# Queries from split operands in a 16-head attention, their weight parts made one layer earlier, and fewer buffers

## The chip, the core and the metric

One core of a Trainium2 chip runs the whole program once. The metric is the device time of one execution in microseconds. PE is the matrix engine, PEld its weight load, DVE, ACT and POOL the vector, scalar and GpSimd engines, SP the engine that issues the DMAs of this kernel.

## What is computed

A residual stream of 4 sequences x 512 tokens x 512 features goes through four pairs of cross-attention and feed-forward; each adds tanh(gate) times its output to the stream. The change touches the third attention and the feed-forward ahead of it. (Beside the third attention the kernel also computes a selective-state recurrence that belongs to the fourth one and doesn't depend on the stream.)

```python
def _L1_ffn_ref(x, w_gate, w_up, w_down):        # ternary weights, 8-bit rows
    gate, up = bitlinear(x, w_gate), bitlinear(x, w_up)
    return h_bitlinear(silu(gate) * up, w_down)  # Hadamard transform of 2048 ahead of it

def _L2_xattn_ref(hidden_states, encoder_hidden_states, Wq, Wk, Wv, Wo, gq, gk):
    q = (hidden_states @ Wq).reshape(B, Sq, H, D)            # H = 16 heads of D = 128
    k = (encoder_hidden_states @ Wk).reshape(B, Skv, H, D)
    v = (encoder_hidden_states @ Wv).reshape(B, Skv, H, D)
    q, k = rmsnorm(q, gq), rmsnorm(k, gk)
    attn = softmax(einsum('bqhd,bkhd->bhqk', q, k) / sqrt(D))
    return einsum('bhqk,bkhd->bqhd', attn, v).reshape(B, Sq, H * D) @ Wo

def step(state, inp):                            # the recurrence, 16 states a channel
    d, b, c, u = inp
    state = state * exp(d[..., None] * A) + (d * u)[..., None] * b[:, None, :]
    return state, einsum('bdn,bn->bd', state, c)
```

## The kernel before

The program is a row of phases (`layer_0`, `l1_xattn`, `l1_ffn`, `l2_xattn`, `moe_and_last`), each with its own buffers, semaphores and one hand-written instruction order per engine; a barrier stands between phases. Every engine runs its list strictly in order, so a wait holds all that follows on that engine. PSUM banks are handed out by `Ring`: jobs take banks in a fixed order, PE fills them, and the job says whether ACT or DVE drains it; a bank is refilled when the job that had it before is drained. Since drains are counted, a wait for one drained job also waits for the jobs of that engine ahead of it in the list.

**The ternary feed-forward, `l1_ffn`.** 16 tiles of 128 tokens go through a pipeline of 19 iterations t (L1591 and the same loop on the other engines). On ACT an iteration does, in this order: copy the turned middle of tile t-1, four SiLUs of tile t (`gate`, L1639), the turned rows of tile t-3 (`y_turned`, L1645), two half copies of tile t-1 (`halves`, L212) and the rounding of tile t-2 (`y_round`). DVE does the Hadamard sums of tile t-2 (`widest`, `rest`, L1734 to L1748), then `middle(t)` and `down(t-3)`, and in every fourth iteration (t = 1, 5, 9, 13) the layer norm for the next sequence, whose power is POOL's only work. SP loads the Hadamard matrix and three weight matrices at the start, waits for two POOL fills, issues one DMA that clears `xs_dram` (L1530; 5888 rows of 513 floats, used two layers later) and waits for it at the end.

**The 16-head attention, `l2_xattn`.** 16 units: 4 sequences x 4 groups of 4 heads (`NU`, `G2`). One iteration u on PE does scores, transposes, values and the output of unit u, and in between the queries, values and keys of units u+1 and u+2 (the order is in the loop that ends the PE block). Keys and values are `split_product`s (L130): both operands are held as a rounded part and a rest in the F32R type, and three products (high x high, high x low, low x high) give one chunk. A query of one head is `product` over 4 chunks in F32: `wq` (1 MB a unit) times `xt`, the transposed normed stream, which `x_turned` copies from PSUM, two chunks by ACT and two by DVE, once for a sequence. ACT squares each query into `q_sq`, copies it to `qt`; the norms follow from a product with ones.

Beside it runs the recurrence, 16 steps (states) a unit: ACT makes `decay`, POOL `inflow` (L2393) and the sum over states (`add_state`, L2405 and L2409), DVE the scan (L2279) and the product with C (`gather`, L2288), and at the end of a unit `skip_term` (L2294), which runs in the next unit behind gather 1. States lie in a circle of `KEPT` = 8 buffers, sums in 2. SP issues two broadcast rows a step, and between them the loads of weights, all on one queue; `inverse` holds two buffers of softmax reciprocals.

Of the kernel before, what the change touches and what calls it, by code (L numbers as in the profile page):

```python
# [5 lines left out]
F32 = mybir.dt.float32  # L6
# [7 lines left out]
P = 128  # L14
# [1457 lines left out]
def l1_ffn(nc, g, a):  # L1472

    with Phase(nc, "l1f") as ph:
# [14 lines left out]
        top = sb("top", [P, 1])  # L1489

# [22 lines left out]
        empty_made, emptied, top_made = sem("empty_made"), sem("emptied"), sem("top_made")  # L1513
        ln = LayerNorm(g, sem)
# [95 lines left out]
        def _(act):  # L1610
# [226 lines left out]
def l2_xattn(nc, g, a):  # L1837

    with Phase(nc, "l2x") as ph:
        sem, sb = ph.sem, ph.sb  # L1840
        wq, wo = [sb(n, [P, DC, D]) for n in ("wq", "wo")]
        wkv = sb("wkv", [P, 2, CC, D], F32R)
        gains = sb("gains", [P, 3])
        ctx_t, xt = sb("ctx_t", [P, 2, CC, S], F32R), sb("xt", [P, DC, S])
        k_tok, v_tok = sb("k_tok", [P, ST, D]), sb("v_tok", [P, ST, D])
        k_sq, q_sq = sb("k_sq", [P, S]), sb("q_sq", [P, 4, S])
# [4 lines left out]
        ot, inv_b = sb("ot", [P, 4, S]), sb("inv_b", [P, 2, S])  # L1851
# [5 lines left out]
        y_sum = sb("y_sum", [P, 2, S])  # L1857
# [12 lines left out]
        b_in, c_in = [[sem(f"{n}_in{k}") for k in range(3)] for n in "bc"]  # L1870
        ln = LayerNorm(g, sem)
# [11 lines left out]
        def _(sp):  # L1883
            def weight(w, name, u, arrived, rows=False):
                cols = slice((u % G2) * D, (u % G2 + 1) * D)
                src = a[name][cols, :] if rows else a[name][:, cols]
                sp.dma_start(w[:], src.rearrange("(c p) n -> p c n", p=P)).then_inc(arrived, 16)
# [41 lines left out]
            weight(wq, "l2_wq", 0, wq_in)  # L1929
# [8 lines left out]
            weight(wo, "l2_wo", 0, wo_in, rows=True)  # L1938
            ring.wait_filled(sp, 0, "q0_3")
            weight(wq, "l2_wq", 1, wq_in)  # L1940
            ring.wait_filled(sp, 0, f"v0_{ST - 1}")
            key_weight(1)
            for u in range(NU):
                for n in range(NS):
                    if n == 3 and u >= 1:
                        ring.wait_filled(sp, 0, f"out{u - 1}_{ST - 1}")
                        weight(wo, "l2_wo", u, wo_in, rows=True)
                    if n == 5 and u >= 1:
                        store_y(u - 1)
                    if n == 8 and u + 1 < NU:  # L1950
                        load_dt(u + 1)
                        load_u(u + 1)
                    if n == 6 and u + 1 < NU:
                        ring.wait_filled(sp, 0, f"k{u + 1}_{ST - 1}")
                        value_weight(u + 1)
                    if n == 10 and u + 2 < NU:
                        ring.wait_filled(sp, 0, f"q{u + 1}_3")
                        weight(wq, "l2_wq", u + 2, wq_in)
# [12 lines left out]
        def _(pe):  # L1971
# [50 lines left out]
            def query(u, h):  # L2022
                if u < NU:
                    pe.wait_ge(wq_in, (u + 1) * 16)
                    ring.wait_for(pe, 0, free=f"q{u}_{h}", drained=[f"xt{u // G2}_{c}" for c in (2, 3)])
                    ring.fill(product(pe, bank(f"q{u}_{h}"), [(wq[:, c, h * P:(h + 1) * P], xt[:, c, :])
                                                              for c in range(DC)]))
# [51 lines left out]
        def _(act):  # L2079
# [25 lines left out]
            def context(u, n, out):  # L2105
                if u < NU:
                    for t in range(ST):
                        ring.wait_filled(act, 0, f"{n}{u}_{t}")
                        if n == "k":
                            for h in range(4):  # L2110
                                cols = slice(h * P, (h + 1) * P)
                                act.activation(k_sq[:, cols], bank(f"k{u}_{t}")[:, cols], ACT.Square,
# [22 lines left out]
            def inverse(u, h):  # L2135
                if u >= 0:
                    ring.wait_filled(act, 0, f"iv{u}_{h}")
                    if u or h >= 2:
                        before = f"pv{u}_{h - 2}" if h >= 2 else f"pv{u - 1}_{h + 2}"
                        ring.wait_for(act, 0, drained=[before])  # L2140
                    copy(act, "act", ring, f"iv{u}_{h}", inv_b[:, h % 2, :], bank(f"iv{u}_{h}"))
# [57 lines left out]
        def _(dve):  # L2199
# [26 lines left out]
            def value(u, h):  # L2226
                if u >= 0:
                    ring.wait_filled(dve, 0, f"pv{u}_{h}")
                    ring.wait_for(dve, 0, drained=[f"iv{u}_{h}"])
                    ring.drain(dve.tensor_tensor(ot[:, h, :], bank(f"pv{u}_{h}"), inv_b[:, h % 2, :], ALU.mult),  # L2230
# [59 lines left out]
            def skip_term(u):  # L2290
                if u >= 0:
                    dve.wait_ge(added, (u + 1) * NS)
                    tile = u_in[:, u % 2, :]
                    dve.scalar_tensor_tensor(tile, tile, g["skip"][:, u % G2:u % G2 + 1], y_sum[:, u % 2, :], ALU.mult,  # L2294
# [65 lines left out]
        def _(pool):  # L2360
# [34 lines left out]
            def add_state(u, n):  # L2395
# [5 lines left out]
                total = y_sum[:, u % 2, :]  # L2401
# [1328 lines left out]
def program(nc, a):  # L3730
    with ExitStack() as stack:
        def sb(name, shape, dt=F32):
# [14 lines left out]
            "kv_dram": nc.dram_tensor("l2x_kv_dram", [3, 4, P, 2 * CC * S], F32).ap(),  # L3747
            "tern_dram": nc.dram_tensor("l1f_tern_dram", [3, P, 4 * I1], BF16).ap(),
# [74 lines left out]
```

## Time and profile before

| | us |
|---|---|
| median of 3 runs | 3502.61 (3500.46 to 3504.72) |
| the profiled execution | 3490.28 |
| its span, first to last instruction | 3488.6 |
| PE busy in the span | 3122.0 |
| DVE busy | 2621.1 |
| ACT busy | 1844.0 |
| POOL busy | 1443.2 |

The ternary feed-forward takes the stretch from about 1077 to 1448 us, the attention that from about 1449 to 2780 us. A timeline row has the start, the duration, the engine, the line, the operation, what it writes and reads, and the count of merged instructions; in brackets stands how long the engine was idle before it, and what ended that.

### The profile page before, as it was taken

What the parts mean: (1) busy time and instruction counts of PE and PEld (TensorE: products, weight loads), DVE (VectorE), ACT (ScalarE), POOL (GpSimd) and SP (SyncE); (2) the same over time, 40 slices, a digit from 0 to 9 for tenths busy, and PEclk for the clock granted to TensorE, in tenths of its full rate; (3) what the DMA queues carried; (4) which work ended last, traced back from release to release, by engine and by line L of the source; (5) the groups of instructions that cost most, each with busy time, mean ns of one, the idle gap of its engine ahead of it and who ended that gap; (6) DMA issues with size and microseconds to landing.
All of it is one profiled execution on the core that took longest, in us unless ns stands there. A gap on an engine that the chain in (4) does not pass through costs nothing. (4 is left out here: it accounts for less than half of the span.)

```text
span 3488.6 us, 42689 instructions
## 1 busy us (share of the span) xinstructions
PE 3122.0 (89%) x14213; PEld 1833.0 (53%) x14244; DVE 2621.1 (75%) x3478; ACT 1844.0 (53%) x3430; POOL 1443.2 (41%) x957
## 2 busy tenths in 40 slices
PE   7869797999997888799999999999999787998985
PEld 3437554333334555455555555555555366786663
DVE  7855689877774888468888888887788864765886
ACT  5644343666663655565666666666656432664220
POOL 1122279000000000067777777777778654223430
PEclk9879899999998999899999999999999898999998
DMA  4137735222216400245555555455454346675421
GB/s 133 40 118 277 277 103 151 58 58 58 64 32 150 63 1 1 85 153 155 182 170 167 162 189 168 154 169 180 159 171 144 127 182 211 249 254 192 145 73 60
DMA packets 229749, 478.66 MB, mean 137 GB/s; under 512 B 36239, under 2 KB 69647, under 8 KB 213664
## 3 DMA queue, kind: packets, MB, share of 16 engines
q1 hardware_dynamic: 223296, 459.19, 41.2%
q0 software_dynamic: 6240, 16.81, 1.3%
q8 instruction: 113, 1.85, 0.2%
q14 instruction: 100, 0.82, 0.1%
HBM read 387.51 MB, written 92.06 MB: 137 GB/s over the span
## 5 line engine op out<-in xcount | busy, mean ns | idle before, releaser
L2393 POOL TENSOR_TENSOR l2x_inflow<-l2x_dtu,l2x_rows_b 128x512 f32<-128x512 f32 x256 | 437.2, 1708 | 254.8 <-DVE l2x_state L2279 253.5
L178 POOL TENSOR_TENSOR ln_work<-ln_work,minus_half 128x4 f32<-128x4 f32 (+1 forms) x34 | 33.1, 975 | 1000.4 <-DVE ln_work L166 1000.3
L2279 DVE TENSOR_TENSOR_SCAN l2x_state<-l2x_decay,l2x_inflow 128x512 f32<-128x512 f32 x256 | 403.9, 1578 | 0.0
L2409 POOL TENSOR_TENSOR l2x_y_sum<-l2x_y_sum,l2x_state 128x512 f32<-128x512 f32 x224 | 387.0, 1728 | 29.2 <-DVE l2x_state L2288 29.2
L1324 DVE TENSOR_REDUCE l1x_mx<-psum 128x2 f32<-128x1024 f32 x256 | 308.4, 1219 | 96.6 <-PE psum L1166 95.2
L1281 ACT ACTIVATE l1x_split<-psum 128x1024 f32<-128x1024 f32 x256 | 262.0, 1025 | 155.6 <-PE psum L1166 155.6
L2288 DVE TENSOR_TENSOR l2x_state<-l2x_state,l2x_rows_c 128x512 f32<-128x512 f32 x256 | 298.2, 1165 | 7.1
L2151 ACT ACTIVATE l2x_decay<-l2x_dt,a_neg 128x512 f32<-128x512 f32 x256 | 181.6, 721 | 165.5 <-DVE l2x_state L2279 165.1
L126 PE MATMUL psum<-l2x_probs_t,l2x_v_tok 128*128 128x512 f32 x512 | 236.3, 605 | 16.1 <-ACT l2x_qt L212 12.9
L126 PE MATMUL psum<-l2x_xt,l2x_wq 128*128 128x512 f32 x512 | 231.9, 597 | 8.6 <-issue 8.6
L2086 ACT ACTIVATE l2x_probs<-psum,l2x_soft,l2x_norms 128x512 f32<-128x512 f32 x256 | 195.6, 774 | 79.9 <-DVE l2x_soft L2218 79.9
L126 PE MATMUL psum<-l2x_kt,l2x_qt 128*128 128x512 f32 x512 | 228.7, 593 | 0.9 <-DVE x_res L218 0.9
L126 PE MATMUL psum<-l2x_wo,l2x_ot 128*128 128x512 f32 x512 | 222.5, 592 | 0.9 <-DVE l2x_ot L2230 0.9
L126 PE MATMUL psum<-l2x_wkv,l2x_ctx_t 128*128 128x512 f32 x768 | 199.1, 415 | 8.8 <-DMA l2x_wkv<-l2x_kv_dram 8.8
L2211 DVE TENSOR_REDUCE l2x_soft<-psum 128x1 f32<-128x512 f32 x256 | 163.5, 681 | 34.9 <-PE psum L126 34.7
L126 PEld LDWEIGHTS psum<-l2x_wkv,l2x_ctx_t 128*128 128x128 f32 x768 | 146.4, 191 | 55.7 <-issue 13.9
L1190 PE MATMUL psum<-l1x_split,l1x_v 128*32 128x256 f32 x2048 | 164.2, 393 | 2.4 <-ACT l1x_o_sb L212 1.3
L126 PEld LDWEIGHTS psum<-l2x_xt,l2x_wq 128*128 128x128 f32 x512 | 96.3, 191 | 126.0 <-issue 125.8
L126 PEld LDWEIGHTS psum<-l2x_wo,l2x_ot 128*128 128x128 f32 x512 | 96.0, 190 | 116.5 <-issue 116.5
L126 PEld LDWEIGHTS psum<-l2x_probs_t,l2x_v_tok 128*128 128x128 f32 x512 | 93.2, 192 | 115.9 <-issue 93.5
L126 PEld LDWEIGHTS psum<-l2x_kt,l2x_qt 128*128 128x128 f32 x512 | 94.4, 190 | 103.6 <-issue 91.6
L119 PEld LDWEIGHTS psum<-ident,l2x_probs 128*128 128x128 f32 x1024 | 115.9, 143 | 47.5 <-issue 37.0
(459 smaller groups left out, 7147.5 us busy)
## 6 DMA issues: line engine op xcount, KB each, us to landing
l2x_rows_b<-l3x_xd_dram SPq DMA_DIRECT2D x256, 256.0 KB, 3.9
l2x_rows_c<-l3x_xd_dram SPq DMA_DIRECT2D x256, 256.0 KB, 3.5
l2w_raw<-l_w SPq DMA_DIRECT2D x38, 1024.0 KB, 6.7
l2x_wkv<-l2x_kv_dram SPq DMA_DIRECT2D x32, 1024.0 KB, 6.8
l2w_raw<-l_w SPq DMA_DIRECT2D x38, 512.0 KB, 4.7
l1x_heads_dram<-l1x_stage SPq DMA_DIRECT2D x32, 512.0 KB, 3.3
l2x_wq<-l_wq SPq DMA_DIRECT2D x16, 1024.0 KB, 5.1
l2x_wo<-l_wo SPq DMA_DIRECT2D x16, 1024.0 KB, 7.3
```

The lines of the kernel that those rows point to most:

```text
L119: last = pe.transpose(bank[:, k * P:(k + 1) * P], tile, ident)
L126: last = pe.matmul(out, lhsT, rhs, start=(k == 0), stop=(k == len(pairs) - 1))
L1190: last = pe.matmul(bank(f"o{gg}", outr)[32 * j:32 * j + 32, cols], v[:, gg // NG, kt, h * VW:h * VW + 2 * HD], probs[:, kt % 2, j, cols], ...
L1281: main.drain(act.activation(probs[:, kt % 2, 2 * j:2 * j + 2, :], g["psum"][:, b:b + 2, :], ACT.Exp, scale=HD ** -0.5), f"{job}_0", banks=2)
L1324: main.drain(dve.tensor_reduce(mx[:, gg % 2, :, j, t], g["psum"][:, b:b + 2, :], AX.X, ALU.max), f"m{n}_0", banks=2)
L2086: ring.drain(act.activation(probs[:, h % 2, t, :], bank(f"s{u}_{h}_{t}"), ACT.Exp, bias=soft[:, h, 1, t:t + 1], scale=norms[:, u % 2, 1, h ...
L2151: act.activation(decay[:, s % 3, :], dt[:, u % 2, :], ACT.Exp, scale=g["a_neg"][:, u % G2, n:n + 1]).then_inc(decay_ready, 1)
L2211: dve.tensor_reduce(soft[:, h, 0, t:t + 1], bank(f"s{u}_{h}_{t}"), AX.X, ALU.max, negate=True).then_inc(max_ready, 1)
L2279: dve.tensor_tensor_scan(state[:, s % KEPT, :], decay[:, s % 3, :], inflow[:, s % 3, :], 0.0, ALU.mult, ALU.add).then_inc(scan_done, 1)
L2288: dve.tensor_tensor(tile, tile, rows_c[:, s % 3, :], ALU.mult).then_inc(gathered, 1)
L2393: pool.tensor_tensor(inflow[:, s % 3, :], dtu[:], rows_b[:, s % 3, :], ALU.mult).then_inc(inflow_ready, 1)
L2409: pool.tensor_tensor(total, total, state[:, s % KEPT, :], ALU.add).then_inc(added, 1)
```

## The change

In the attention `wq` and `xt` become split operands: twice the bytes, three F32R products for a chunk instead of one in F32. ACT copies all four chunks of `xt` as the rounded part, and DVE subtracts to get the rest. The parts of the query weights are made in `l1_ffn`: SP loads raw weights in 8 pieces of 512 KB, ACT rounds a piece in each odd iteration behind `gate`, POOL subtracts (behind the power of the layer norm), and SP stores both parts to DRAM (1 MB a piece), from where the attention loads 2 MB a unit. The raw loads are issued behind the clearing of `xs_dram`. States are kept in 3 buffers instead of 8, sums in 1 instead of 2 (the first addition of a unit now waits for the skip term of the unit just before), reciprocals in 1 instead of 2 (its copy waits for the product of the head before), and the squares of keys use a row of `q_sq`.

```diff
 # l1_ffn
+        q_raw, q_parts = sb("q_raw", [P, 2, 2, D]), sb("q_parts", [P, 2, 2, D], F32R)
 ...
         def _(sp):
             sp.dma_start(g["xs_dram"].rearrange("(j p) d -> p j d", p=P),
                          empty[:].unsqueeze(1).to_broadcast([P, 2 * NP, ROW])).then_inc(emptied, 16)
+            def query_weight(p):
+                m, half = divmod(p, 2)
+                rows = slice(half * 2 * P, (half + 1) * 2 * P)
+                sp.dma_start(q_raw[:, p % 2], a["l2_wq"][rows, m * D:(m + 1) * D].rearrange("(c p) n -> p c n", p=P)
+                             ).then_inc(q_in[p % 2], 16)
+            def query_parts(p):
+                m, half = divmod(p, 2)
+                sp.wait_ge(q_lo, p + 1)
+                sp.dma_start(g["wq_dram"][m, :, :, 2 * half:2 * half + 2, :], q_parts[:].bitcast(F32)).then_inc(q_stored, 16)
+            query_weight(0)
+            query_weight(1)
+            for p in range(2 * G2):
+                query_parts(p)
+                if p + 2 < 2 * G2:
+                    query_weight(p + 2)
             sp.wait_ge(emptied, 16)
+            sp.wait_ge(q_stored, 2 * G2 * 16)
 ...
         def _(act):
+            def query_high(p):
+                act.wait_ge(q_in[p % 2], (p // 2 + 1) * 16)
+                if p:
+                    act.wait_ge(q_stored, p * 16)
+                act.activation(q_parts[:, 0], q_raw[:, p % 2], ACT.Copy).then_inc(q_hi, 1)
 ...
                     gate(t)
+                if t % 2 and t // 2 < 2 * G2:
+                    query_high(t // 2)
                 if 0 <= t - 3 < T1:
                     y_turned(t - 3)
 ...
         def _(pool):
+            def query_low(p):
+                pool.wait_ge(q_hi, p + 1)
+                pool.tensor_tensor(q_parts[:, 1], q_raw[:, p % 2], q_parts[:, 0].bitcast(F32), ALU.subtract
+                                   ).then_inc(q_lo, 1)
             for b in range(NB):
                 ln.pool(pool, b)
+                query_low(2 * b)
+                query_low(2 * b + 1)
 # l2_xattn
-KEPT = 8
+KEPT = 3
 ...
-        turned = [(f"xt{u // G2}_{c}", "act" if c % 2 else "dve") for c in range(DC)] if u % G2 == 0 and u < NU else []
+        turned = [(f"xt{u // G2}_{c}", "dve") for c in range(DC)] if u % G2 == 0 and u < NU else []
 ...
-        ot, inv_b = sb("ot", [P, 4, S]), sb("inv_b", [P, 2, S])
+        ot, inv_b = sb("ot", [P, 4, S]), sb("inv_b", [P, S])
 ...
-        y_sum = sb("y_sum", [P, 2, S])
+        y_sum = sb("y_sum", [P, S])
 ...
-                    ring.fill(product(pe, bank(f"q{u}_{h}"), [(wq[:, c, h * P:(h + 1) * P], xt[:, c, :])
-                                                              for c in range(DC)]))
+                    ring.fill(split_product(pe, bank(f"q{u}_{h}"), [
+                        ([wq[:, k, c, h * P:(h + 1) * P] for k in range(2)], [xt[:, k, c, :] for k in range(2)])
+                        for c in range(DC)]))
 ...
             def x_turned(u):                                  # ACT
-                    for c in (1, 3):
+                    for c in range(DC):
                         ring.wait_filled(act, 0, job)
-                        copy(act, "act", ring, job, xt[:, c, :], bank(job))
+                        act.activation(xt[:, 0, c, :], bank(job), ACT.Copy).then_inc(xt_hi, 1)
 ...
             def inverse(u, h):                                # ACT
-                    if u or h >= 2:
-                        before = f"pv{u}_{h - 2}" if h >= 2 else f"pv{u - 1}_{h + 2}"
-                        ring.wait_for(act, 0, drained=[before])
+                    if u or h:
+                        ring.wait_for(act, 0, drained=[f"pv{u}_{h - 1}" if h else f"pv{u - 1}_3"])
 ...
             def x_turned(u):                                  # DVE
-                    for c in (0, 2):
-                        ring.wait_filled(dve, 0, job)
-                        copy(dve, "dve", ring, job, xt[:, c, :], bank(job))
+                    for c in range(DC):
+                        dve.wait_ge(xt_hi, u // G2 * DC + c + 1)
+                        ring.drain(dve.tensor_tensor(xt[:, 1, c, :], bank(job), xt[:, 0, c, :].bitcast(F32),
+                                                     ALU.subtract), job)
 ...
             def add_state(u, n):                              # POOL
                 if n == 1:
-                    since(pool, y_read, u - 1)
+                    since(pool, y_read, u)
 ...
+            "wq_dram": nc.dram_tensor("l2x_wq_dram", [G2, P, 2, DC, D], F32).ap(),
```

## Rows read from the trace of the kernel before

**Rows 1.** page, busy us of each engine, its share of the span, instructions
```profile
PE 3122.0 (89%) x14213; PEld 1833.0 (53%) x14244; DVE 2621.1 (75%) x3478; ACT 1844.0 (53%) x3430; POOL 1443.2 (41%) x957
```

**Rows 2.** busy time by engine in one attention stretch; PEclk, DMA share, GB/s
```profile
2065.00:2143.00 78.00, 77.09 (x279) 42.76 (x278) 63.38 (x72) 48.88 (x125) 59.00 (x36) 1.00 0.53 171
```

**Rows 3.** groups by shape, 1450 to 2800 us: count, busy, mean ns, idle
```profile
L126 PE MATMUL psum<-l2x_xt,l2x_wq 128*128 128x512 f32 x512 | 231.9, 597 | 8.6 <-issue 8.6
...
L126 PE MATMUL psum<-l2x_wkv,l2x_ctx_t 128*128 128x512 f32 x768 | 199.1, 415 | 8.8 <-DMA l2x_wkv<-l2x_kv_dram 8.8
```

**Rows 4.** timeline of PE, one unit: start us, us, line, out<-in, count
```profile
2059.45 6.16 PE L126 MATMUL psum<-l2x_wkv,l2x_ctx_t 128*128 128x512 f32 x24
2065.45 7.03 PE L126 MATMUL psum<-l2x_kt,l2x_qt 128*128 128x512 f32 x16
2072.31 3.60 PE L126 MATMUL psum<-l2x_xt,l2x_wq 128*128 128x512 f32 x8
2075.75 1.91 PE L119 MATMUL psum<-ident,l2x_probs 128*128 128x128 f32 x16
...
2082.44 3.70 PE L126 MATMUL psum<-l2x_probs_t,l2x_v_tok 128*128 128x512 f32 x8 [0.91 <-ACT l2x_qt L212]
...
2111.05 1.06 PE L2033 MATMUL psum<-l2x_q_sq,ones 128*32 128x512 f32 x8
```

**Rows 5.** waits, 1450 to 2800 us: total us, times, longest
```profile
PE psum L126 <- ACT l2x_qt L212: 12.9, 14, 1.0
```

**Rows 6.** timeline of ACT, copy of query 3 in the same unit
```profile
2109.05 0.60 ACT L212 ACTIVATE l2x_qt<-psum 128x512 f32<-128x512 f32 x1
```

**Rows 7.** timelines of DVE and POOL at the start of the next unit
```profile
2155.03 1.23 DVE L2279 TENSOR_TENSOR_SCAN l2x_state<-l2x_decay,l2x_inflow 128x512 f32<-128x512 f32 x1
...
2156.90 1.76 DVE L2294 SCALAR_TENSOR_TENSOR l2x_u_in<-l2x_u_in,skip,l2x_y_sum 128x512 f32<-128x512 f32 x1
...
2161.60 2.20 DVE L2279 TENSOR_TENSOR_SCAN l2x_state<-l2x_decay,l2x_inflow 128x512 f32<-128x512 f32 x1
...
2158.07 1.72 POOL L2405 TENSOR_TENSOR l2x_y_sum<-l2x_state 128x512 f32<-128x512 f32 x1
```

**Rows 8.** DMA issues at the layer's start: count, KB, us to landing
```profile
l2x_wq<-l_wq SPq DMA_DIRECT2D x1, 1024.0 KB, 10.5
```

**Rows 9.** SP's timeline and its landing, ternary layer
```profile
1080.40 0.45 SPq L1530 DMA_DIRECT2D l2f_xs_dram<-l1f_empty  x1
...
l2f_xs_dram<-l1f_empty SPq DMA_DIRECT2D x1, 11799.0 KB, 102.6
```

**Rows 10.** SP's timeline and landings, key weights and the rows behind
```profile
2043.18 0.44 SPq L1894 DMA_DIRECT2D l2x_wkv<-l2x_kv_dram  x1
2043.67 0.43 SPq L1918 DMA_DIRECT2D l2x_rows_b<-l3x_xd_dram  x1
...
l2x_wkv<-l2x_kv_dram SPq DMA_DIRECT2D x1, 1024.0 KB, 6.9
...
l2x_rows_b<-l3x_xd_dram SPq DMA_DIRECT2D x1, 256.0 KB, 8.2
```

**Rows 11.** timelines of ACT and DVE, second tile of the ternary layer
```profile
1108.40 0.69 ACT L1639 ACTIVATE l1f_silu<-psum,l1f_xs 128x512 f32<-128x512 f32 x1 [1.04 <-PE psum L126]
1110.15 0.60 ACT L212 ACTIVATE l1f_half<-psum 128x512 f32<-128x512 f32 x1 [1.07 <-PE psum L1574]
...
1116.78 0.69 DVE L1734 TENSOR_TENSOR l1f_z<-psum,l1f_half 128x512 f32<-128x512 f32 x1
```

**Rows 12.** groups by shape: another split of weights, POOL and ACT
```profile
L2999 POOL TENSOR_TENSOR l2w_w_lo<-l2w_raw,l2w_w_hi 128x1024 fp32r<-128x1024 f32 x1 | 2.5, 2517 | 0.0
...
L2717 ACT ACTIVATE l2w_w_hi<-l2w_raw 128x1024 fp32r<-128x1024 f32 x1 | 1.0, 1040 | 0.0
```

**Rows 13.** timelines of ACT and DVE, a later tile of the ternary layer
```profile
1237.17 1.94 ACT L1645 ACTIVATE l1f_yt<-psum 128x1024 bf16<-128x1024 bf16 x2 [0.62 <-PE psum L1583]
...
1242.91 0.75 DVE L1759 SCALAR_TENSOR_TENSOR x_res<-psum,l1f_ys,x_res 128x512 f32<-128x512 f32 x1 [1.94 <-PE psum L126]
```

More of the change, by code:

```diff
@@ L1513, in l1_ffn @@
         empty_made, emptied, top_made = sem("empty_made"), sem("emptied"), sem("top_made")
+        q_hi, q_lo, q_stored = sem("q_hi"), sem("q_lo"), sem("q_stored")
+        q_in = [sem(f"q_in{k}") for k in range(2)]
         ln = LayerNorm(g, sem)
@@ L1840, in l2_xattn @@
         sem, sb = ph.sem, ph.sb
-        wq, wo = [sb(n, [P, DC, D]) for n in ("wq", "wo")]
+        wq, wo = sb("wq", [P, 2, DC, D], F32R), sb("wo", [P, DC, D])
         wkv = sb("wkv", [P, 2, CC, D], F32R)
         gains = sb("gains", [P, 3])
-        ctx_t, xt = sb("ctx_t", [P, 2, CC, S], F32R), sb("xt", [P, DC, S])
+        ctx_t, xt = sb("ctx_t", [P, 2, CC, S], F32R), sb("xt", [P, 2, DC, S], F32R)
         k_tok, v_tok = sb("k_tok", [P, ST, D]), sb("v_tok", [P, ST, D])
-        k_sq, q_sq = sb("k_sq", [P, S]), sb("q_sq", [P, 4, S])
+        q_sq = sb("q_sq", [P, 4, S])
         qt, kt = sb("qt", [P, 4, S]), sb("kt", [P, 4, S])
@@ L1870, in l2_xattn @@
         b_in, c_in = [[sem(f"{n}_in{k}") for k in range(3)] for n in "bc"]
+        xt_hi = sem("xt_hi")
         ln = LayerNorm(g, sem)
@@ L1883, in _, with output_weight, query_weight @@
         def _(sp):
[L1884 to L1887, printed above, removed]
+            def output_weight(u):
+                rows = slice((u % G2) * D, (u % G2 + 1) * D)
+                sp.dma_start(wo[:], a["l2_wo"][rows, :].rearrange("(c p) n -> p c n", p=P)).then_inc(wo_in, 16)
+            def query_weight(u):
+                sp.dma_start(wq[:].rearrange("p h c n -> p (h c n)").bitcast(F32),
+                             g["wq_dram"][u % G2].rearrange("p h c n -> p (h c n)")).then_inc(wq_in, 16)
             def context(b):
@@ L1928, in _ @@
             key_weight(0)
-            weight(wq, "l2_wq", 0, wq_in)
+            query_weight(0)
             for k, n in enumerate(("l2_gq", "l2_gk")):
@@ L1937, in _ @@
             value_weight(0)
-            weight(wo, "l2_wo", 0, wo_in, rows=True)
+            output_weight(0)
             ring.wait_filled(sp, 0, "q0_3")
-            weight(wq, "l2_wq", 1, wq_in)
+            query_weight(1)
             ring.wait_filled(sp, 0, f"v0_{ST - 1}")
@@ L1946, in _ @@
                         ring.wait_filled(sp, 0, f"out{u - 1}_{ST - 1}")
-                        weight(wo, "l2_wo", u, wo_in, rows=True)
+                        output_weight(u)
                     if n == 5 and u >= 1:
@@ L1957, in _ @@
                         ring.wait_filled(sp, 0, f"q{u + 1}_3")
-                        weight(wq, "l2_wq", u + 2, wq_in)
+                        query_weight(u + 2)
                     row_b(u * NS + n + 2)
@@ L2024, in query @@
                     pe.wait_ge(wq_in, (u + 1) * 16)
-                    ring.wait_for(pe, 0, free=f"q{u}_{h}", drained=[f"xt{u // G2}_{c}" for c in (2, 3)])
-                    ring.fill(product(pe, bank(f"q{u}_{h}"), [(wq[:, c, h * P:(h + 1) * P], xt[:, c, :])
-                                                              for c in range(DC)]))
+                    ring.wait_for(pe, 0, free=f"q{u}_{h}", drained=[f"xt{u // G2}_{DC - 1}"])
+                    ring.fill(split_product(pe, bank(f"q{u}_{h}"), [
+                        ([wq[:, k, c, h * P:(h + 1) * P] for k in range(2)], [xt[:, k, c, :] for k in range(2)])
+                        for c in range(DC)]))
             def query_norms(u):
@@ L2111, in context @@
                                 cols = slice(h * P, (h + 1) * P)
-                                act.activation(k_sq[:, cols], bank(f"k{u}_{t}")[:, cols], ACT.Square,
+                                act.activation(q_sq[:, 3, cols], bank(f"k{u}_{t}")[:, cols], ACT.Square,
                                                accum_out=norms[:, u % 2, 2, h, t:t + 1]).then_inc(k_squared, 1)
@@ L2137, in inverse @@
                     ring.wait_filled(act, 0, f"iv{u}_{h}")
-                    if u or h >= 2:
-                        before = f"pv{u}_{h - 2}" if h >= 2 else f"pv{u - 1}_{h + 2}"
-                        ring.wait_for(act, 0, drained=[before])
-                    copy(act, "act", ring, f"iv{u}_{h}", inv_b[:, h % 2, :], bank(f"iv{u}_{h}"))
+                    if u or h:
+                        ring.wait_for(act, 0, drained=[f"pv{u}_{h - 1}" if h else f"pv{u - 1}_3"])
+                    copy(act, "act", ring, f"iv{u}_{h}", inv_b[:], bank(f"iv{u}_{h}"))
             def decays(u, n):
@@ L2229, in value @@
                     ring.wait_for(dve, 0, drained=[f"iv{u}_{h}"])
-                    ring.drain(dve.tensor_tensor(ot[:, h, :], bank(f"pv{u}_{h}"), inv_b[:, h % 2, :], ALU.mult),
+                    ring.drain(dve.tensor_tensor(ot[:, h, :], bank(f"pv{u}_{h}"), inv_b[:], ALU.mult),
                                f"pv{u}_{h}")
@@ L2293, in skip_term @@
                     tile = u_in[:, u % 2, :]
-                    dve.scalar_tensor_tensor(tile, tile, g["skip"][:, u % G2:u % G2 + 1], y_sum[:, u % 2, :], ALU.mult,
+                    dve.scalar_tensor_tensor(tile, tile, g["skip"][:, u % G2:u % G2 + 1], y_sum[:], ALU.mult,
                                              ALU.add).then_inc(y_read, 1)
@@ L2400, in add_state @@
                 s = u * NS + n
-                total = y_sum[:, u % 2, :]
+                total = y_sum[:]
                 pool.wait_ge(gathered, s + 1)
                 if n == 1:
-                    since(pool, y_read, u - 1)
+                    since(pool, y_read, u)
                     pool.tensor_tensor(total, state[:, (s - 1) % KEPT, :], state[:, s % KEPT, :], ALU.add
```

## The prediction

> **What bounds the kernel now.** I read the page's first part first: PE is busy for 89% of the span, DVE for 75% [rows 1]. That is a mean over six layers, and the change touches two of them, so the next view is busy time by stretch. In the sixteen-head attention (about 1449 to 2780 us) a 78 us stretch holds 77.1 us of PE, 63.4 of DVE, 48.9 of ACT and 59.0 of POOL at a granted clock of 1.0 [rows 2]. So PE sets the pace there. The groups by shape say what PE does: the query product is 512 instructions, the key and value products, which already use split operands, 768 [rows 3]. The timeline of PE then gives the true pace, because busy times of pipelined matmuls overlap: it is the distance between starts. The list of waits says where PE itself stands still. For the ternary feed-forward (1077 to 1448 us) I read the timelines of ACT and DVE, and the DMA issues with their landings, because the change puts transfers and waits there.
>
> **The query product.** One head is now 4 products in full precision, 8 instructions; from its start at 2072.31 to the next group at 2075.75 it takes 3.44 us [rows 4]. A split product of the same shape is 24 instructions from 2059.45 to 2065.45, 0.250 us each [rows 4]. A query head becomes 12 of these, 3.00 us: 0.44 us less for each of 64 heads, 28 us if all of it counted. The price could be lower (2048 columns in 3.44/4 = 0.86 us is 0.215 us for one pass of 512 columns; 12 of them are 2.58 us) or higher (the group's busy time, 199.1/768 = 0.259 us, gives 3.11); I take 0.250, the same product beside it.
>
> Not all of it counts. A unit (4 heads of one batch) runs on PE in this order: scores 0 and 1, query 0, transposes, query 1, value 0, ..., query 2, score 3, query 3, value 2, norms. At value 0 PE already waits 0.91 us, for the copy of query 0 out of PSUM [rows 4]; over the layer this is 12.9 us in 14 waits [rows 5]. ACT comes to that copy late not because of the query but because it has to finish the second exponential, the decay and four copies of transposes first, and these hang on DVE's maxima and scans since the first score. Shorter queries 0 and 1 therefore only lengthen this wait. Queries 2 and 3 come after it: 0.88 us a unit counts, if the next wait holds. That is the norms, which need the copy of query 3: its row starts at 2109.05 and takes 0.60 us, PE arrives at 2111.05 [rows 4, 6]. A slack of 1.4 us covers 0.88. If ACT were later there, the saving would shrink by what is missing. Four heads of the first unit, before any attention, count in full: 1.8 us. The other 15 units with a query: 15 x 0.88 = 13.2 us. Sum: -15.0 us, bounds 0 and -28.
>
> **Three states, one sum, one reciprocal buffer.** With three states, the scan of step n waits until POOL has added state n-3. POOL's order is inflow n, then this addition, and the scan waits for inflow n anyway, so at most one addition of 1.7 us is new. Steady steps have several us in hand; the tight place is the start of a unit: scan 3 waits for the first addition (both first states in one), which with one sum must also wait for the skip term of the unit before. The skip term ends at 2156.90 + 1.76 = 2158.66, the addition starts at 2158.07 now; it would end at about 2158.7 + 1.7 = 2160.4, and scan 3 starts at 2161.60 [rows 7]. Slack 1.2 us: I cost it at nothing. Without that slack it costs up to one addition in each of 16 units, 28 us, on DVE, where the maxima, the reciprocals and so the wait at value 0 are queued behind the scan. The reciprocal buffer's copy waits for the DVE product of the head before, and an exponential or a query copy stands between the two on ACT: nothing. Key squares go to a buffer that nobody reads then: nothing. The split of x adds two ACT copies and turns DVE copies into four subtractions, three times in the steady part; DVE is later by about 1 us, and it waits for PE there afterwards. At the start of the layer it stands on the path: the first weight load lands 10.5 us after its issue [rows 8], with twice the bytes about 1 us more (it is now contiguous, like the key weights) to 4 us (as now, doubled). I take +1. Later loads of 2 MB push the broadcast rows behind them back further than now; these rows are asked for two steps ahead, so I take nothing, up to 1 us a unit if that is not enough.
>
> **What is put into the ternary layer.** SP issues the clearing of the routed rows (11.8 MB) at 1080.40, and it lands 102.6 us later, at 1183.0 [rows 9]. The two first loads of raw query weights are issued right behind it, on the same queue. What the queue does with a small transfer behind a large one is to be seen in the attention layer: key weights issued at 2043.18 land after 6.9 us, at 2050.1; 256 KB of rows issued 0.5 us later land after 8.2 us, at 2051.9, 1.8 us behind them though they have a quarter of the bytes [rows 10]. So the first raw weights land at about 1183.0 + 1.8 = 1184.8, 104 us after their issue. The Trainium skill says the same of one engine ("DMA: Bandwidth & Descriptors", Queues, rings and completion order): descriptors are consumed in ring order, and it adds that completion is not in order for a whole queue when transfers use different numbers of engines; both transfers here have 128 partitions, which by that page of the Trainium skill is all 16 engines, so it leaves no way past.
>
> ACT waits for these weights in tile 1, behind its last activation before the wait, 1108.40 + 0.69 = 1109.1, and everything that ACT does afterwards is queued behind the wait: the two half copies, the first now at 1110.15, which DVE's first Hadamard sums need [rows 11]. DVE has other work until 1116.78, so the first 5 us cost nothing. After the change: landing 1184.8, the rounded copy 1.04 [rows 12], two half copies 2 x 0.60 [rows 11] and 0.3 for the hand-overs (an estimate), so DVE goes on at 1187.3 instead of 1116.78. Stall: **+70.5 us**, bounds 69 and 73. Nothing runs beside it that would be saved later: PE's four banks are full, DVE has nothing.
>
> After it, eight times one rounded copy on ACT of 1.04 us and one subtraction on POOL of 2.52 us [rows 12]. ACT has 0.62 us of idle before the next activation and the path goes on from there to the down product, for which DVE waits 1.94 us [rows 13]: about 0.4 us counts, 7 x 0.4 = +2.8 (bounds 0 and 7 x 1.04). POOL's subtraction can hold DVE: a scan takes 1.23 us by itself and 2.20 next to a POOL operation of half this length [rows 7], so about 2.1 us here. In tiles 5, 9 and 13 it starts with the layer norm's last step, on DVE's path: +6.4. In the other tiles it falls beside DVE's products from PSUM and the 1.94 us of idle behind them, which takes up nearly all of it [rows 13], and in tile 1 beside the stall. Bounds 0 and 7 x 2.1 = 15. The Trainium skill speaks against this part of the change too ("SBUF — State Buffer", Terms): VectorE and GpSimd share a port pair, and whoever comes second waits for the other's whole instruction. By that rule the three tiles would cost an estimated 3 x 2.52 = 7.6 us and the sum would be 1.2 us more; the scan's stretch of 0.97 us beside an operation of about 1.7 us is less than the rule's, and this layer has no POOL work yet to show it.
>
> **Sum.** 70.5 + 2.8 + 6.4 + 1.0 - 15.0 = +65.7 us. The profiled execution took 3490.3 us (span 3488.6), so 3556.0 by it. The runs shown have a median of 3502.6, 0.35% above the profiled one; the same difference on it gives **3568**.
>
> **Rivals.**
> *The transfers pass each other.* If the 16 engines share themselves out so that the raw weights land before 1109, there is no stall: 3568 - 70.5 = 3498, within 0.2% of before, and 3491 if POOL's subtraction doesn't hold DVE either, faster. It decides at one point, the landing of the first 512 KB, 28 us or 104 us after its issue. For it: an engine that is done with its share of the clearing can take up the weights early. Against it: the rows behind the key weights [rows 10], and a landing that counts only when every engine is done. 0.12.
> *All of the query time counts*, because DVE and ACT follow PE more closely at value 0 than I think: 15 x 0.88 more, 3555. Against it: 14 waits of 16 at that place. 0.08.
> *The short ring of states becomes the bound*: an addition of 1.73 us in each of 16 units, 3596. For it: slack of only 1.2 us. 0.08.
> *The change doesn't do what it says*: above 0.287 us a split matmul costs what it replaces, 3583. Against it: 0.250 for the key product. 0.04.
>
> **How the numbers follow.** My forecast has 0.68, the rivals 0.32. A measurement of this kernel can tell some 0.2%, 7 us, from no change. The first rival's 0.12 goes to faster 0.05, same 0.05 and slower 0.02 (shares partly, a shorter stall); all else is slower. The range takes in the bounds of the ternary layer and of the queries, and the second to fourth rivals: 3545 to 3598; only the first rival and the far tails are outside.
>
> **What would show it.** In the profile after, ACT's first rounded copy in the ternary layer waits for a DMA for some 75 us and starts at about 1184.8; the clearing still lands at 1183; DVE resumes at about 1187. The query group has 768 instructions, PE's wait at value 0 grows from 0.9 to about 1.8 us, the unit shrinks by 0.9 us, and scan 3 waits for nothing on POOL. A first copy that starts before 1110 makes the prediction wrong at once; a wait in front of scans or of the norms makes the size wrong.

## The result and the profile after

| | before | after |
|---|---|---|
| median, us | 3501.53 (4 runs, 3495.48 to 3504.72) | 3555.93 (4 runs, 3553.94 to 3580.97) |
| profiled execution, its span | 3490.28, 3488.6 | 3554.87, 3553.1 |
| ternary layer: first DMA issue to that of the attention | 371.13 | 452.80 |
| attention: first DMA issue to that of the next layer | 1335.61 | 1318.96 |

The changed kernel is slower: ratio 1.0174, 95% interval 1.0127 to 1.0221. The profiled executions lie 64.6 us apart. The two layers together account for 81.67 - 16.65 = 65.0 of it, so nothing else moved. The ends of the two stretches are these issues of SP in the changed kernel (start us, us):

```profile
1077.12 0.34 SPq L1529 DMA_DIRECT2D l1f_had<-hadamard  x1
...
1529.92 0.35 SPq L1931 DMA_DIRECT2D l2x_ctx_t<-l2x_kv_dram  x1
...
2848.88 0.50 SPq L2603 DMA_DIRECT2D l2w_raw<-l_w  x1
```

In the ternary layer, the timelines of SP, ACT and DVE of the changed kernel:

```profile
1080.34 0.45 SPq L1533 DMA_DIRECT2D l2f_xs_dram<-l1f_empty  x1
1080.84 77.23 SPq L1539 DMA_DIRECT2D l1f_q_raw<-l_wq  x2
...
1108.22 0.69 ACT L1661 ACTIVATE l1f_silu<-psum,l1f_xs 128x512 f32<-128x512 f32 x1 [1.04 <-PE psum L126]
1187.15 1.06 ACT L1682 ACTIVATE l1f_q_parts<-l1f_q_raw 128x1024 fp32r<-128x1024 f32 x1 [78.24 <-DMA l1f_q_raw<-l_wq]
...
1189.21 0.69 DVE L1764 TENSOR_TENSOR l1f_z<-psum,l1f_half 128x512 f32<-128x512 f32 x1 [72.53 <-ACT l1f_half L212]
```

ACT's first rounding waits 78.24 us for raw weights issued directly behind the clearing. DVE, which resumed at 1116.78 before [rows 11], resumes at 1189.21. With the layer's start 0.24 us earlier, this stall is 1189.21 - 1116.78 + 0.24 = 72.7 us. In tiles 5, 9 and 13 POOL's subtraction meets the layer norm's last step; in tile 5 of the changed kernel:

```profile
1271.10 2.34 POOL L1817 TENSOR_TENSOR l1f_q_parts<-l1f_q_raw,l1f_q_parts 128x1024 fp32r<-128x1024 f32 x1
1271.27 3.82 DVE L171 TENSOR_SCALAR xn<-x_res,ln_work 128x512 f32<-128x512 f32 x4 [1.22 <-POOL ln_work L178]
```

In the attention, the timeline of PE over the unit that answers to [rows 4], and the list of waits that answers to [rows 5] (total us, times, longest):

```profile
2134.56 6.16 PE L126 MATMUL psum<-l2x_wkv,l2x_ctx_t 128*128 128x512 f32 x24
2140.56 7.03 PE L126 MATMUL psum<-l2x_kt,l2x_qt 128*128 128x512 f32 x16
2147.02 3.36 PE L126 MATMUL psum<-l2x_xt,l2x_wq 128*128 128x512 f32 x12
2150.22 2.04 PE L119 MATMUL psum<-ident,l2x_probs 128*128 128x128 f32 x16
...
2157.55 3.70 PE L126 MATMUL psum<-l2x_probs_t,l2x_v_tok 128*128 128x512 f32 x8 [1.68 <-ACT l2x_qt L212]
...
2166.71 3.60 PE L126 MATMUL psum<-l2x_probs_t,l2x_v_tok 128*128 128x512 f32 x8
2169.74 3.37 PE L126 MATMUL psum<-l2x_xt,l2x_wq 128*128 128x512 f32 x12
2172.95 1.91 PE L119 MATMUL psum<-ident,l2x_probs 128*128 128x128 f32 x16
...
2184.89 1.06 PE L2075 MATMUL psum<-l2x_q_sq,ones 128*32 128x512 f32 x8
```
```profile
PE psum L126 <- ACT l2x_qt L212: 23.5, 15, 1.7
PE psum L2075 <- ACT l2x_qt L212: 3.3, 5, 1.4
```

From the value weights' product to value 0 it is 2157.55 - 2134.56 = 22.99 us, exactly as before (2082.44 - 2059.45, [rows 4]): two queries in between became shorter, and the wait for ACT grew from 0.91 to 1.68 us. From value 0 to the norms it is 27.34 us instead of 28.61. Most units without new `xt` take 78.26 us instead of 79.55.

### The profile page after: what moved, and what is told of

Its sections match the earlier page's. It is cut to its first block and busy times, and to the rows that moved or that the text cites. A ratio compares the mean times of both kernels' runs of the same rounds, so it can differ in the third digit from the quotient of the medians.

```text
span 3553.1 us, 43289 instructions
## 1 busy us (share of the span) xinstructions
PE 3093.5 (87%) x14500; PEld 1883.2 (53%) x14500; DVE 2626.6 (74%) x3486; ACT 1853.3 (52%) x3446; POOL 1467.2 (41%) x965
## 5 line engine op out<-in xcount | busy, mean ns | idle before, releaser
L2321 DVE TENSOR_TENSOR_SCAN l2x_state<-l2x_decay,l2x_inflow 128x512 f32<-128x512 f32 x256 | 384.3, 1501 | 0.3 <-issue 0.3
L2330 DVE TENSOR_TENSOR l2x_state<-l2x_state,l2x_rows_c 128x512 f32<-128x512 f32 x256 | 317.3, 1239 | 7.1
L126 PE MATMUL psum<-l2x_xt,l2x_wq 128*128 128x512 f32 x768 | 211.2, 425 | 13.3 <-issue 9.2
L126 PEld LDWEIGHTS psum<-l2x_xt,l2x_wq 128*128 128x128 f32 x768 | 145.7, 192 | 69.6 <-issue 39.3
L119 PE MATMUL psum<-ident,l1f_mid 128*128 128x128 f32 x256 | 42.6, 315 | 123.5 <-ACT l1f_half L212 76.2
```

Of the source, the lines that this page charges most:

```text
L119: last = pe.transpose(bank[:, k * P:(k + 1) * P], tile, ident)
L126: last = pe.matmul(out, lhsT, rhs, start=(k == 0), stop=(k == len(pairs) - 1))
L2321: dve.tensor_tensor_scan(state[:, s % KEPT, :], decay[:, s % 3, :], inflow[:, s % 3, :], 0.0, ALU.mult, ALU.add).then_inc(scan_done, 1)
L2330: dve.tensor_tensor(tile, tile, rows_c[:, s % 3, :], ALU.mult).then_inc(gathered, 1)
```

## The experiments

The theory: the loss is one wait, made by the order of transfers on SP's queue. The main rival: the clearing takes the DMA engines' time in any order. For the attention: behind value 0 the time of the queries counts, ahead of it not; the small buffers cost nothing. Each experiment's lengths of the two layers are read between the same issues as above.

### The raw loads ahead of the clearing

```diff
+            query_weight(0)
+            query_weight(1)
             sp.wait_ge(empty_made, 2)
             sp.dma_start(g["xs_dram"]...).then_inc(emptied, 16)
-            query_weight(0)
-            query_weight(1)
             for p in range(2 * G2):
                 query_parts(p)
```

> The changed kernel with the two first raw loads issued ahead of the clearing of the routed rows, on the same queue; nothing else is different. Theory (order on SP's queue): the first rounding on ACT waits for nothing, the 72 us are gone, but the store of the first parts is issued behind the clearing and lands at about 1187, and the second rounding, whose place without a stall is 1150, waits for it. DVE has some 5 us of other work, so about 32 us come back there: 3555 - 72 + 32 = 3515. Rival (the clearing takes the DMA engines' whole time, whatever the order): the loads still land near 1185 and the time stays at 3555. Rival (the wait isn't what costs): 3555 too, with the loss in another place.

Measured: one execution of 3538.16 us. ACT's and SP's timelines:

```profile
1115.36 1.05 ACT L1681 ACTIVATE l1f_q_parts<-l1f_q_raw 128x1024 fp32r<-128x1024 f32 x1
1191.22 1.06 ACT L1681 ACTIVATE l1f_q_parts<-l1f_q_raw 128x1024 fp32r<-128x1024 f32 x1 [32.84 <-DMA l2x_wq_dram<-l1f_q_parts]
```
```profile
1086.05 0.48 SPq L1546 DMA_DIRECT2D l2f_xs_dram<-l1f_empty  x1
1123.52 36.59 SPq L1541 DMA_DIRECT2D l2x_wq_dram<-l1f_q_parts  x1
```

The first rounding waits for nothing; the second waits 32.84 us, because the store it needs was issued behind the clearing. The ternary layer takes 418.2 us, 37.4 more than without any such wait (380.9, two experiments below; forecast 32) and 34.6 less than in the changed kernel. The rival falls: the same bytes in another order cost half. The total of 3515 was missed by 23 us. 5 of them are this layer's; most of the others fall where the edit doesn't reach: against the profiled execution of the changed kernel, this one came to the ternary layer 4.7 us later, took 7.0 us more in the expert layer behind the attention (158.9 and 152.0) and 5.0 in what follows it.

### The clearing on ACT's queue

```diff
 # SP
-            sp.wait_ge(empty_made, 2)
-            sp.dma_start(g["xs_dram"]...).then_inc(emptied, 16)
 # ACT, ahead of x_round(0)
+            act.wait_ge(empty_made, 2)
+            act.dma_start(g["xs_dram"]...).then_inc(emptied, 16)
```

> The changed kernel with the clearing issued by ACT on its own queue, at the start of the layer; raw loads and stores of parts stay on SP's. The clearing moves the same 11.8 MB over the same DMA engines, only the queue is another. Theory (order on SP's queue): the first raw weights land well before 1109, no stall: 3555 - 72 = 3483, some 0.5% faster than before. Rival (the clearing takes the engines' time, whatever the queue): raw weights land near 1183, 3555. In between, if the engines share their time by turns between queues, the first load takes some 10 to 20 us, which is still before 1109.

Measured: median 3495.17 us (10 runs, 3487.01 to 3514.0) beside 3500.3 for the kernel before (23 runs); ratio 0.9989, interval 0.9974 to 1.0005. The profiled execution took 3487.0. ACT's timeline, and the DMA queues from 1099 to 1103 us, where the first raw load moves (packets, MB, share of the 16 engines' time; q10 is ACT's queue, q1 SP's):

```profile
1080.08 0.42 ACTq L1688 DMA_DIRECT2D l2f_xs_dram<-l1f_empty  x1
...
1112.62 1.05 ACT L1678 ACTIVATE l1f_q_parts<-l1f_q_raw 128x1024 fp32r<-128x1024 f32 x1
```
```profile
q10 hardware_dynamic: 315, 0.65, 52.5%
q1 hardware_dynamic: 304, 0.56, 46.5%
```

By the packets in the trace (2052 bytes each in the clearing, 2048 in a raw load), the clearing runs from 1082.3 to 1184.6, and the first raw load passes from 1099.3 to 1102.7, some 20 us after its issue at 1082.67. The same bytes cross the same engines in the same stretch, from another queue, and no rounding waits. So the queue's order made the stall, not the bandwidth. The Trainium skill ("DMA: Bandwidth & Descriptors", Queues, rings and completion order) says that each DMA engine takes turns between its queues, packet by packet. These rows agree: the two queues had 315 and 304 packets in the same 4 us. A price of the sharing isn't shown: the layer takes 383.0 us here, and 380.9, 383.0 and 382.4 in three executions with the clearing in pieces (the next kernel and the last two). The forecast of 3483 was missed by 4 us by the profiled execution and by 12 by the median; why the ten runs spread over 27 us stays open.

### The clearing in eight pieces

`clear(p)` issues an eighth of the clearing.

```diff
-            sp.dma_start(g["xs_dram"]...).then_inc(emptied, 16)
 ...
             for p in range(2 * G2):
                 query_parts(p)
                 if p + 2 < 2 * G2:
                     query_weight(p + 2)
+                clear(p)
```

> The changed kernel with the clearing cut into 8 pieces of 1.5 MB (12.8 us each by the 102.6 us of the whole), each issued on SP's queue behind the next raw load, so that no raw load or store has more than one piece ahead of it. Theory: no stall, 3483, as with the clearing on ACT's queue. Rival (a load behind a piece comes too late for its rounding): some us for each of eight pieces; the pieces are two tiles, about 40 us, apart, so this should not show.

Measured: median 3487.53 us (8 runs, 3484.0 to 3496.3), ratio 0.9962, interval 0.9951 to 0.9973. No rounding waits for a DMA; the ternary layer takes 380.86 us, the attention 1319.96. The stall is the whole difference between a loss of 1.7% and a gain of 0.4%.

### The small buffers alone

```diff
 # the kernel before
-KEPT = 8
+KEPT = 3
-        y_sum = sb("y_sum", [P, 2, S])
+        y_sum = sb("y_sum", [P, S])
-        ot, inv_b = sb("ot", [P, 4, S]), sb("inv_b", [P, 2, S])
+        ot, inv_b = sb("ot", [P, 4, S]), sb("inv_b", [P, S])
```

> The kernel before with the buffers of the change alone: three states for eight, one running sum, one reciprocal buffer; queries and the ternary layer are as before. Theory: nothing, within 0.2% of before, scans wait for nothing on POOL. Rival (the short ring binds): an addition of 1.7 us in each of 16 units, +28 us or 0.8%.

Measured: median 3503.23 us (10 runs), ratio 1.0012, interval 1.0000 to 1.0024. The groups of scans and first additions (busy us, mean ns, idle ahead of them):

```profile
L2278 DVE TENSOR_TENSOR_SCAN l2x_state<-l2x_decay,l2x_inflow 128x512 f32<-128x512 f32 x256 | 398.6, 1557 | 0.0
...
L2404 POOL TENSOR_TENSOR l2x_y_sum<-l2x_state 128x512 f32<-128x512 f32 x16 | 32.6, 2037 | 10.8 <-DVE l2x_u_in L2293 10.8
```

The scans wait for nothing. POOL now waits 10.8 us in all for the skip terms, and its first additions are slower (2037 ns for 1746 before); nobody waits for that: the ternary layer takes 371.0 us as before, the attention 1333.7, 1.9 less. The 28 us of the rival are excluded; a cost up to 0.24% isn't by the runs alone, but these two layers show none.

### Two moves in the version without the stall

```diff
-                if t % 2 and t // 2 < 2 * G2:
+                if t % 2 == 0 and t // 2 < 2 * G2:
                     query_high(t // 2)
 # POOL
             for b in range(NB):
-                ln.pool(pool, b)
                 query_low(2 * b)
+                ln.pool(pool, b)
                 query_low(2 * b + 1)
 # DVE, attention: x_turned(0) ahead of the wait for the gains
-            dve.wait_ge(gains_in, 32)
             ...
             x_turned(0)
+            dve.wait_ge(gains_in, 32)
```

> The kernel with the clearing split (its profiled run: ternary layer 380.9 us from its first issue to the next layer's, attention 1320.0), with two moves. First, the roundings go into the even tiles, and POOL subtracts before the layer norm of a batch, not behind it. Theory (POOL's subtraction stretches the layer norm's last step on DVE by 1.9 us in tiles 5, 9 and 13, ACT's rounding costs the rest): the three jumps of 2.0 us are gone and the layer takes about 374.8 us; the 0.3 us for each rounding stays. Rival (the subtraction holds DVE wherever it stands): still about 381. Second, at the start of the attention DVE makes the low halves of x before it waits for the gains, which land behind the 2 MB of query weights. Theory: PE's first query starts when the weights are there and not behind DVE's wait, some 1.5 to 2 us earlier. Rival (the weights themselves land as late): 0. Sum by theory: 6 + 1.5 to 2 us less, near 3480, 0.6% faster than before.

Measured: median 3475.27 us (5 runs, 3472.23 to 3481.9), ratio 0.9925, interval 0.9911 to 0.9939: the best of all here. DVE's layer norm step in tile 5 and PE's first queries, both in this version, and the windows of the first queries in the version with the clearing split and in this one (us, busy time and count by engine, granted clock, DMA share, GB/s):

```profile
1198.47 1.91 DVE L171 TENSOR_SCALAR xn<-x_res,ln_work 128x512 f32<-128x512 f32 x4 [1.22 <-POOL ln_work L178]
...
1465.46 11.36 PE L126 MATMUL psum<-l2x_xt,l2x_wq 128*128 128x512 f32 x48
```
```profile
1476.60:1480.00 3.40, 3.40 (x10) 2.69 (x11) 0.00 (x0) 0.33 (x1) 3.13 (x2) 0.64 0.91 349
```
```profile
1465.50:1478.00 12.50, 11.33 (x49) 8.78 (x47) 0.00 (x0) 10.25 (x32) 3.35 (x3) 1.00 0.57 197
```

The ternary layer takes 374.0 us, 6.9 less than in the profiled execution with the pieces, where, without the stall, the subtraction had stretched the step in tile 1 too. The step is back at 1.91 us, and what stays against before is 374.0 - 371.1 = 2.9 us for eight roundings and subtractions. The first query starts 14.4 us after the first transposes of x instead of 16.6 (2.2 less), and the norms come 3.8 us earlier: ahead of the query group PE no longer waits 2.00 us, and the group runs at a granted clock of 1.00, not 0.64 in its first 3.4 us. Over the whole attention 4.4 us are gone (1315.5 for 1320.0), where 1.5 to 2 were forecast; this and a start of the ternary layer 2.0 us earlier, which the edit doesn't reach, put the median 5 us below the forecast of 3480.

### Shorter queries ahead of the wait, and behind it

```diff
-                    ring.fill(split_product(...))
+                    parts = [(wq[:, m, c, ...], xt[:, k, c, :]) for c in range(DC)
+                             for m, k in (((0, 0), (0, 1)) if h < 2 else ((0, 0), (0, 1), (1, 0)))]
+                    ring.fill(product(pe, bank(f"q{u}_{h}"), parts))
```

> The kernel with the clearing split, whose queries of heads 0 and 1 leave out the product of the weights' low part with x's high part: 8 matmuls for 12. Each of these two heads takes 4 x 0.25 = 1.0 us less on PE. Theory (PE waits at value 0 for ACT's copy of query 0, whose chain doesn't depend on the length of the query): the wait grows from 1.7 to about 3.7 us and the unit stays at 78.26. Only the first unit, with nothing beside it, may gain up to 2 us. Rival (all of the query time counts): 2.0 us a unit, 76.3, and 30 us over 15 units.

For heads 2 and 3 the edit has `h >= 2`:

> The same omission in heads 2 and 3 alone. Theory (these lie behind the wait): query 2 counts in full, 1.0 us, because score 3 and with it DVE's maxima, the third exponential and the copy of query 3 come earlier too; of query 3 only the slack in front of the norms counts, 0.5 us by the changed kernel's rows (ACT's copy ends at 2184.4, the norms start at 2184.9). So a unit takes 78.26 - 1.5 = 76.8 us, and PE waits for ACT's copy of query 3 in every unit, about 0.5 us. Rival (value 0 isn't special, ACT alone sets the unit): 0 here too. Rival (PE alone sets it): 2.0 us a unit, 76.3.

Both are single executions (3496.05 and 3497.01 us) and are read within the attention alone. Measured with heads 0 and 1: the norms of the first unit come 1.9 us earlier, as the expectation allowed. From norms to norms, most units in which the clock holds take 78.26 to 78.28 us, as without the omission. PE waits 2.61 us at value 0, and in most units 0.84 us for an exponential ahead of it. Six of the fifteen units got longer, by 0.7 to 3.1 us and by 11.0 together. PE's timeline at value 0 in two units, the first of them one of the six, and the windows of that one:

```profile
2093.39 5.36 PE L126 MATMUL psum<-l2x_probs_t,l2x_v_tok 128*128 128x512 f32 x8 [2.61 <-ACT l2x_qt L212]
...
1852.38 3.70 PE L126 MATMUL psum<-l2x_probs_t,l2x_v_tok 128*128 128x512 f32 x8 [2.61 <-ACT l2x_qt L212]
```
```profile
2090.50:2093.30 2.80, 0.28 (x3) 0.04 (x1) 2.77 (x4) 2.77 (x7) 2.80 (x2) 1.00 0.61 176
2093.40:2096.00 2.60, 2.60 (x3) 1.16 (x4) 2.57 (x2) 2.57 (x5) 2.60 (x2) 0.50 0.69 205
```

So queries 0 and 1 don't count, as predicted; taking PE work away there even cost. In the six longer units the granted clock was 0.54 to 0.72 on the mean over these eight matmuls, in the other nine 1.00. With full queries, behind a wait of at most 1.69 us, it was 1.00 in all fifteen. The attention took 1329.0 us, 9 more than with full queries.

Measured with heads 2 and 3: the shortest units take 77.89 us, only 0.37 less, the whole attention 1318.9 us, 1.1 less, and PE waits 1.4 us or more at the norms in every unit. My 1.5 us were wrong. PE's timeline, and DVE's ahead of it:

```profile
2116.22 2.43 PE L126 MATMUL psum<-l2x_xt,l2x_wq 128*128 128x512 f32 x8
...
2123.95 1.06 PE L2080 MATMUL psum<-l2x_q_sq,ones 128*32 128x512 f32 x8 [1.43 <-ACT l2x_qt L212]
```
```profile
2113.08 1.70 DVE L2326 TENSOR_TENSOR_SCAN l2x_state<-l2x_decay,l2x_inflow 128x512 f32<-128x512 f32 x1
2114.81 1.58 DVE L2335 TENSOR_TENSOR l2x_state<-l2x_state,l2x_rows_c 128x512 f32<-128x512 f32 x1
2116.32 2.47 DVE L2257 TENSOR_REDUCE l2x_soft<-psum 128x1 f32<-128x512 f32 x4
2118.82 0.16 DVE L2264 TENSOR_TENSOR l2x_soft<-l2x_soft,l2x_norms 128x4 f32<-128x4 f32 x1
```

Score 3 does come 0.95 us earlier behind value 0, but DVE takes up its maxima only behind a scan and a gather, at 2116.32. That is 19.3 us behind the start of value 0 with and without the omission. The exponential, the copy of query 3 and the norms hang on that. The changed kernel stands within 0.4 us of DVE's pace in this half of the unit, so a still shorter query would bring no more.

## Why the prediction was right, step by step

Forecast 3568, range 3545 to 3598, slower with 0.9; measured 3555.93. The sum against the profiled execution gave 3556.0, and the profiled execution after took 3554.87.

| step | forecast | measured |
|---|---|---|
| stall behind the clearing | +70.5 | +72.7 |
| POOL holding DVE, tiles 5, 9, 13 | +6.4 | +6.1 |
| roundings on ACT | +2.8 | +2.9 |
| 15 later units | -13.2 | -17.9 |
| start of the attention with its first unit | +1.0 - 1.8 | +2.4 |
| behind the last norms | 0 | -1.2 |
| sum | +65.7 | +65.0 |

**The stall** came as told, at the place and by the mechanism; reordering and another queue confirm it. The term was 2.2 us small because the rounding started at 1187.15, not 1184.8. By the packets in the two traces the clearing's last one ended at 1185.4, before at 1182.3. Packets of the raw loads had moved since 1154.7, so they did start while others of the clearing were still to come, as was said for the first rival; but the rounding started only at 1187.15, behind the clearing's last packet.

**POOL's hold** came out at 2.02, 2.04 and 2.02 us a time (the growth of the shift between the two traces in tiles 6, 10 and 14). The size was partly luck: the prediction took it from a scan beside "a POOL operation of half this length" [rows 7], but the operation that ran beside that scan took 1.77 us, 0.7 of 2.52. What holds DVE is seen in tile 5: the subtraction starts at 1271.10 and lasts 2.34 us; the step beside it starts 0.17 us later, and the first of its four instructions takes 2.45 us instead of 0.55 and ends 0.28 us behind the subtraction, while the other three hardly change (0.53 and 0.54). The Trainium skill ("SBUF — State Buffer", Terms) says that whoever comes second at the shared port pair is blocked for the other's full instruction. These rows agree. The prediction's 7.6 us by that rule took three whole subtractions of 2.52 us; 2.34 - 0.17 = 2.17 us were left of each, 6.5 together, and 6.1 were lost.

**The queries: right mechanism, wrong size.** The step that was mis-sized is "3.44 - 3.00 = 0.44 us a head", by the price of 0.250 us an instruction. I took the split product from its own start to the next start. Within a group its matmuls start 0.233 us apart (48 in a row in the fifth experiment: the last starts 10.97 us behind the first), which is 2.80 us for 12 and 5.60 for the 24 whose distance was 6.00. The other 0.40 us belong to the F32 group ahead: F32 matmuls start 0.43 us apart, but the first of the 24 has its start 0.03 us behind the last F32 one. Taken from the start of the F32 group ahead to the start of the group behind, value 1 and query 2 are 2172.95 - 2166.71 = 6.24 us, and before they were 2098.47 - 2091.60 = 6.87: 0.63 us a head. The rows of before for this:

```profile
2091.60 3.60 PE L126 MATMUL psum<-l2x_probs_t,l2x_v_tok 128*128 128x512 f32 x8
2095.04 3.60 PE L126 MATMUL psum<-l2x_xt,l2x_wq 128*128 128x512 f32 x8
2098.47 1.91 PE L119 MATMUL psum<-ident,l2x_probs 128*128 128x128 f32 x16
```

Two heads behind the wait give 1.26 of the 1.29 us seen. The unit's whole gain lies there; queries 0 and 1 gave nothing, as forecast, and the wait grew to 1.68 us, forecast about 1.8. That the norms would hold was nearly wrong: in four units behind a turn of x PE waits 0.3 to 0.7 us there.

**The start of the attention** failed: +2.4 instead of -0.8. I counted later weights, and missed that DVE's subtractions of x stand behind its wait for the gains, two loads of 512 bytes behind the 2 MB on SP's queue. DVE and PE after, and PE before:

```profile
1544.73 0.21 DVE L2244 TENSOR_SCALAR l2x_gains<-l2x_gains 128x1 f32<-128x1 f32 x1 [15.70 <-DMA l2x_gains<-l_gk]
1544.98 2.48 DVE L2285 TENSOR_TENSOR l2x_xt<-psum,l2x_xt 128x512 fp32r<-128x512 f32 x4
1547.61 12.97 PE L126 MATMUL psum<-l2x_xt,l2x_wq 128*128 128x512 f32 x48 [2.87 <-DVE l2x_xt L2285]
```
```profile
1462.99 13.89 PE L126 MATMUL psum<-l2x_xt,l2x_wq 128*128 128x512 f32 x32
```

The first query starts 1547.61 - 1530.12 = 17.5 us after the first transposes of x, before 1462.99 - 1448.68 = 14.3: 3.2 us later. The four shorter queries gave 0.8 us of that back instead of 1.8. The norms' wait for ACT at their end isn't the reason, 1.44 us now and 1.31 before. The clock is: behind the wait of 2.87 us it was granted at 0.51 in the first 3.4 us of the group, and at 1.00 before. In the fifth experiment, at 1.00, the group takes 11.36 us for 13.89, 2.5 less, which is 4 x 0.63. That experiment took the gains' wait away and got 3.8 us back.

**The last step, 0.35% on top**, failed too: I put the median 12 us above the sum because the three runs of before stood that far above its profiled execution. After, they differ by 1.1 us (3555.93 and 3554.87). What lies behind the attention, the same code in all nine traces, took from 704.0 to 716.2 us in them, and 704.5 and 704.2 in those of before and after: the profiled execution of before was a short one there, and so was that of after. The medians lie 54.4 us apart, the profiled executions 64.6; the interval of the ratio, 44 to 77 us, holds both. The errors of the units (-4.7) and of the start and end (+2.0) and the stall (+2.2) nearly cancel, so the sum is better than its parts.

**The rivals.** Transfers that pass each other: no, on one queue; on two queues yes, and then the time is near what that rival gave (3498 by my offset, 3485.5 without it; measured a median of 3495.2 and a profiled 3487.0, and 3487.5 and 3487.7 with the pieces on one queue). All of the query time counts: no. The ring of states: no; in the changed kernel the 256 scans wait 0.3 us in all. The change doesn't do what it says: no, a split head takes up 2.81 us of PE (3.44 - 0.63) and not 3.44.

## What to carry to other kernels

A small load that an engine waits for must not be issued behind a large transfer on the same queue: cut the large one, put it behind, or issue it from another queue. An off-path step put into an engine's list is only as harmless as its latest input. Price a pipelined group from the start of the group ahead to the start of the group behind, and ask for each saving which engine is next: here 0.63 us a head counted in two heads of four, and 0.4 us more was all that was left.

## What the runs showed of the hardware

- The issue itself is held: two issues of SP behind the 11.8 MB clearing took 77.23 us together, of which the first took 73.20 (the usual one takes 0.61). SP issued nothing else in that time. The clearing's own issue, ahead of them, took 0.45 us, and from ACT 0.42.
- A wait of PE of 2.6 us was followed, in six of fifteen units, by eight matmuls that took 5.1 to 6.8 us instead of 3.70; in the one shown the granted clock was 0.50, the lower of the two levels (1.2 GHz), in their first 2.6 us. In the other nine they took 3.70 behind the same wait, at 1.00. What decides between them stays open.
- A chunk of 128x128 by 512 takes up 0.70 us of PE as three F32R products (0.233 us each) and 0.86 us as one in F32 (two matmuls 0.43 us apart). Read from a group's own start behind an F32 group, 12 F32R matmuls look like 3.21 us (2172.95 - 2169.74) instead of 2.80.
